# Second graph layer: one-hot matrix on ScalarE, feature halves paired on VectorE, one head-sum matmul per block, and programs written out

## The reference

```python
enh = node_features + 0.1 * query_emb[None, :]
Q = (enh @ Wq + bq).reshape(N, H, D)
K = (enh @ Wk + bk).reshape(N, H, D)
V = (enh @ Wv + bv).reshape(N, H, D)
rel = rel_w[edge_relations]
mod_k = K[src] + 0.2 * rel[:, None, :]
scores = jnp.einsum('ehd,ehd->eh', Q[dst], mod_k) / D ** 0.5
seg_max = jax.ops.segment_max(scores, dst, num_segments=N)
ex = jnp.exp(scores - seg_max[dst])
denom = jax.ops.segment_sum(ex, dst, num_segments=N)
w = ex / denom[dst]
agg = jax.ops.segment_sum(w[:, :, None] * V[src], dst, num_segments=N)
```

## Time and profile before

| | |
|---|---|
| median of 3 runs | 1894.05 us (1893.74 to 1898.3) |
| the profiled execution | 1896.89 us, span 1895.1 us |
| busy in the span | PE 88%, DVE 85%, ACT 55%, POOL 55% |
| TensorE's granted clock, mean | 0.943 of full speed |
| DMA | 333.74 MB, mean 176 GB/s |

### The profile page before, as it was taken

How to read it: one execution, slowest core, us unless ns; L and a number is a source line. 1 busy time by engine, 2 the same in 40 slices (tenths; PEclk the granted TensorE clock), 3 DMA queues, 4 the chain that set the end, 5 groups by cost and what they waited for, 6 DMA issues and landing times. The chain is left out here.

```text
span 1895.1 us, 46044 instructions
## 1 busy us (share of the span) xinstructions
PE 1660.5 (88%) x11647; PEld 1543.2 (81%) x11647; DVE 1617.6 (85%) x3652; ACT 1047.8 (55%) x2325; POOL 1040.0 (55%) x1079
## 2 busy tenths in 40 slices
PE   6979999999999999996096999889899899899844
PEld 3779999999999999996085888788788788788633
DVE  5569999999999999999874799888888788888887
ACT  1468888888888888885453444343343343343114
POOL 0056666666566666665714766565565565565164
PEclk6989999999999999998598999999999999999978
DMA  4466666666666666662227877576576576676513
GB/s 130 153 188 186 185 188 185 185 186 184 188 185 185 186 183 188 184 186 85 98 97 248 251 205 213 169 208 185 170 208 179 170 207 181 178 200 190 195 51 102
DMA packets 165698, 333.74 MB, mean 176 GB/s; under 512 B 31015, under 2 KB 101384, under 8 KB 165092
## 3 DMA queue, kind: packets, MB, share of 16 engines
q0 software_dynamic: 70400, 231.64, 42.6%
q1 hardware_dynamic: 95204, 101.16, 16.9%
HBM read 307.63 MB, written 25.06 MB: 176 GB/s over the span
## 5 line engine op out<-in xcount | busy, mean ns | idle before, releaser
L456 POOL DMA_INDIRECT gath<-edge_in_tab,idx x440 | 464.2, 1055 | 301.3 <-DVE gate_in L864 230.5
L469 POOL DMA_INDIRECT kept_more<-kv_tab,idx x176 | 173.4, 985 | 145.4 <-DVE weighted L1029 87.1
L1128 PE MATMUL bank<-w_lo,relu_hi 128*128 128x256 f32 x880 | 249.4, 283 | 0.0
L1128 PE MATMUL bank<-w_hi,relu_lo 128*128 128x256 f32 x880 | 249.3, 283 | 0.0
L1128 PE MATMUL bank<-w_hi,relu_hi 128*128 128x256 f32 x880 | 249.3, 283 | 0.0
L1128 PE MATMUL bank<-weighted,hot 128*128 128x260 f32 x880 | 238.7, 396 | 4.4 <-DVE agg L1060 4.4
L606 ACT ACTIVATE relu_hi<-bank 128x512 fp32r<-128x512 f32 x220 | 131.7, 599 | 141.6 <-PE bank L1128 141.6
L1128 PEld LDWEIGHTS bank<-weighted,hot 128*128 128x128 f32 x880 | 172.4, 197 | 34.5 <-DVE hot L1038 6.3
L1131 PE MATMUL bank<-ident,gath 128*128 128x128 f32 x880 | 168.8, 274 | 23.9 <-DVE ea_parts L851 13.3
L469 POOL DMA_INDIRECT hs<-kv_tab,idx x132 | 141.9, 1075 | 80.5 <-DVE weighted L1029 47.9
L873 DVE TENSOR_TENSOR msg<-bank,gate 128x512 f32<-128x512 f32 x220 | 152.1, 692 | 33.3 <-PE bank L1128 17.2
(11 more groups left out here) (266 smaller groups left out, 5018.9 us busy)
## 6 DMA issues: line engine op xcount, KB each, us to landing
ea_in<-in_ea SPq DMA_DIRECT2D x440, 64.0 KB
block_row<-row_tab SPq DMA_DIRECT2D x440, 64.0 KB
gath<-edge_in_tab,idx POOLq DMA_INDIRECT x440
kv_tab<-qkv_row SPq DMA_DIRECT2D x26, 258.0 KB, 2.5
edge_in_tab<-node_row SPq DMA_DIRECT2D x26, 256.0 KB, 2.0
xs<-in_x SPq DMA_DIRECT2D x1, 3328.0 KB, 15.5
rows_tab<-xs SPq DMA_DIRECT2D x1, 3328.0 KB, 9.3
rows_tab<-hs SPq DMA_DIRECT2D x1, 3328.0 KB, 10.9
```

What stands on the lines that cost most here:

```text
L456: g.indirect_dma_start(gath[:, q, i, :], None, edge_in_tab, bass.IndirectOffsetOnAxis(ap=idx[:, half, q, i:i + 1], axis=0)).then_inc(gath_ ...
L469: g.indirect_dma_start(kept(u, 0, KVW)[:, i, :], None, kv_tab, bass.IndirectOffsetOnAxis(ap=idx1[:, half, u % BATCH, i:i + 1], axis=0)).th ...
L1128: return nc.tensor.matmul(out_, lhsT=lhs, rhs=rhs, start=start, stop=stop)
```

## The change

Four things in the second layer:

- The features of each head are split in two parts of 32. The columns of Wk, bk, Wq, bq and of the relations are laid out so that half 0 of the keys holds the first parts of all four heads and half 1 the second parts. VectorE then adds half 1 to half 0 (`pair_parts`, 128x256), and `add_heads` is one matmul of 256 columns where it was two. `rel_parts` is filled by 8 instructions of 32 columns on ScalarE and on VectorE each, where it was 4 of 64.
- `hot1` is made by ScalarE in two stages, `node_distances` (Square of the difference, two instructions of 128x128, lag 16) and `one_hot1` (Relu of 1 minus it, 128x256, lag 17), as the first layer does.
- The order within a step is new: on VectorE `rescale` and `add_agg` stand directly behind `products`, then `pair_parts`, then `weight_values`. On TensorE `aggregate` stands ahead of `add_heads`. On ScalarE the copy of the scores is last, and `one_hot1` stands behind the exponents.
- The three pipelines are written out (`straight=True`); those of GpSimd and SyncE stay loops.

```diff
-FIRST_COL = HEADS * BATCH - 2
+FIRST_COL = HEADS * (BATCH - 1)
+PART = HEAD // 2
...
-            for h in range(HEADS):
-                last = s.mul(rel_parts[:, h * HEAD:(h + 1) * HEAD], rel_sb[:], 0.2)
+            for part in range(2):
+                for h in range(HEADS):
+                    last = s.mul(rel_parts[:, part * P + h * PART:part * P + (h + 1) * PART], rel_sb[:, part * PART:(part + 1) * PART], 0.2)
...
+            def node_distances(k, q):
+                b = KEEP * k + q
+                after(act, hot1_done, b - 1)
+                for i in range(2):
+                    last = s.activation(dist1[:, q % 2, i, :], iota_node[:], ACT.Square, bias=rel_col[:, ds(b, 1), i], scale=-1.0)
+                last.then_inc(dist1_done, 1)
+
+            def one_hot1(k, q):
+                b = KEEP * k + q
+                act.wait_ge(dist1_done, b + 1)
+                after(act, agg_ready, b - 1)
+                s.activation(hot1[:, q % 2, :, :], dist1[:, q % 2, :, :], ACT.Relu, bias=one_col[:], scale=-1.0).then_inc(hot1_done, 1)
...
-            pipeline(act, [(fetch_query, 0), (copy_keys, 1), (copy_scores, 2), (copy_weights, 6), (exponents, 5)], BLOCKS, KEEP)
+            pipeline(act, [(fetch_query, 0), (copy_keys, 1), (copy_weights, 6), (exponents, 5), (one_hot1, 17), (node_distances, 16), (copy_scores, 2)],
+                     BLOCKS, KEEP, straight=True)
...
+            def pair_parts(k, q):
+                b = KEEP * k + q
+                dve.wait_ge(prod_done, b + 1)
+                parts = kept(q, 0, CHUNK)
+                v.tensor_tensor(parts[:, 0, :], parts[:, 0, :], parts[:, 1, :], ALU.add).then_inc(paired, 1)
...
-            def one_hot1(k, q):
-                b = KEEP * k + q
-                after(dve, agg_ready, b - 1)
-                for i in range(2):
-                    last = v.tensor_scalar(hot1[:, q % 2, i, :], iota_node[:], rel_col[:, ds(b, 1), i], None, ALU.is_equal)
-                last.then_inc(hot1_done, 1)
...
-            pipeline(dve, [(one_hot_t, 0), (products, 2), (weight_values, 17), (one_hot1, 17), (rescale, 19), (add_agg, 19), (local_maxima, 3),
-                           (running_maxima, 4), (segment_maxima, 5)], BLOCKS, KEEP)
+            pipeline(dve, [(one_hot_t, 0), (products, 2), (rescale, 19), (add_agg, 19), (pair_parts, 2), (weight_values, 17), (local_maxima, 3),
+                           (running_maxima, 4), (segment_maxima, 5)], BLOCKS, KEEP, straight=True)
...
-                pe.wait_ge(prod_done, b + 1)
+                pe.wait_ge(paired, b + 1)
                 if turn == 0:
                     after(pe, scores_copied, g)
-                for c in range(2):
-                    at = FIRST_COL - HEADS * turn - 2 * c
-                    last = mm(bank[4][:, 0:CHUNK], adder[:, at:at + P], kept(q, 0, CHUNK)[:, c, :],
-                              turn == 0 and c == 0, turn == BATCH - 1 and c == 1)
+                at = FIRST_COL - HEADS * turn
+                last = mm(bank[4][:, 0:CHUNK], adder[:, at:at + P], kept(q, 0, CHUNK)[:, 0, :], turn == 0, turn == BATCH - 1)
...
-            pipeline(pe, [(keys_and_queries, 0), (ends_of_rows, 3), (carry_to_rows, 4), (add_heads, 1), (aggregate, 17), (weights_to_columns, 5)],
-                     BLOCKS, KEEP)
+            pipeline(pe, [(keys_and_queries, 0), (ends_of_rows, 3), (carry_to_rows, 4), (aggregate, 17), (add_heads, 1), (weights_to_columns, 5)],
+                     BLOCKS, KEEP, straight=True)
```

More of the change, by code:

```diff
@@ L181, in build @@
                     hot1 = sb(a1, "hot1", [P, 2, 2, P], f32)
+                    dist1 = sb(a1, "dist1", [P, 2, 2, P], f32)
             a3 = ExitStack()
@@ L246, in build @@
         brow_in, kept_in = sems("brow_in", BROWS), sems("kept_in", BATCH)
-        idx1_done, hot_t_done, key_ready, key_copied, query_fetched, query_ready, prod_done, scores_ready = (
+        idx1_done, hot_t_done, key_ready, key_copied, query_fetched, query_ready, prod_done, paired, scores_ready = (
             sem(n) for n in ("idx1_done", "hot_t_done", "key_ready", "key_copied", "query_fetched", "query_ready",
-                             "prod_done", "scores_ready"))
+                             "prod_done", "paired", "scores_ready"))
         far_done, steps_known, steps_out, steps_arrived = sem("far_done"), sem("steps_known"), sem("steps_out"), sems("steps_arrived", 2)
@@ L266, in build @@
         idx_seen, rel_in, rel_done, agg_zero = sem("idx_seen"), sem("rel_in"), sem("rel_done"), sem("agg_zero")
-        segments_known = sem("segments_known")
+        segments_known, dist1_done = sem("segments_known"), sem("dist1_done")
         def after(engine, signal, n):
@@ L491, in _ @@
             step(g.memset(qkv_row[:], 1.0))
-            step(g.memset(adder[0:HEAD, FIRST_COL:FIRST_COL + 1], 1.0))
-            g.memset(adder[HEAD:, FIRST_COL + 1:FIRST_COL + 2], 1.0).then_inc(consts, 1)
+            for h in range(HEADS - 1):
+                step(g.memset(adder[h * PART:(h + 1) * PART, FIRST_COL + h:FIRST_COL + h + 1], 1.0))
+            g.memset(adder[(HEADS - 1) * PART:, FIRST_COL + HEADS - 1:FIRST_COL + HEADS], 1.0).then_inc(consts, 1)
             pool.wait_ge(consts, 2)
@@ L913, in _ @@
             dve.wait_ge(rel_done, 1)
-            for h in range(HEADS):
-                last = v.scalar_tensor_tensor(rel_parts[RELS:, h * HEAD:(h + 1) * HEAD], in0=rel_sb[RELS:, :], scalar=0.2,
-                                              in1=rel_parts[RELS:, h * HEAD:(h + 1) * HEAD], op0=ALU.mult, op1=ALU.subtract)
+            for part in range(2):
+                for h in range(HEADS):
+                    cols = slice(part * P + h * PART, part * P + (h + 1) * PART)
+                    last = v.scalar_tensor_tensor(rel_parts[RELS:, cols], in0=rel_sb[RELS:, part * PART:(part + 1) * PART], scalar=0.2,
+                                                  in1=rel_parts[RELS:, cols], op0=ALU.mult, op1=ALU.subtract)
             last.then_inc(rel_done, 1)
@@ L1370, in col, with halves @@
         return np.ascontiguousarray(np.asarray(a).reshape(2, P).T)
+    def halves(a):
+        a = np.asarray(a)
+        return a.reshape(a.shape[:-1] + (HEADS, 2, PART)).swapaxes(-3, -2).reshape(a.shape)
     x = np.asarray(x)
@@ L1387 @@
         "query_col": col(L1_gnn_query_emb),
-        "wqkv": np.concatenate([np.asarray(a) for a in (L1_gnn_Wk, L1_gnn_Wv, L1_gnn_Wq)], axis=1),
-        "b_qkv": np.concatenate([np.asarray(a) for a in (L1_gnn_bk, L1_gnn_bv, L1_gnn_bq)])[None, :],
+        "wqkv": np.concatenate([halves(L1_gnn_Wk), np.asarray(L1_gnn_Wv), halves(L1_gnn_Wq)], axis=1),
+        "b_qkv": np.concatenate([halves(L1_gnn_bk), np.asarray(L1_gnn_bv), halves(L1_gnn_bq)])[None, :],
         "rel": np.asarray(L1_gnn_rel_w),
```

## The result

The changed kernel takes 1783.7 us (median of 4 runs, 1778.23 to 1786.45) against 1894.81 us (4 runs, 1893.74 to 1898.3) for the kernel before on the same chip: ratio 0.9407, 95% interval 0.9381 to 0.9433. The forecast was 1800 us, range 1776 to 1842; the gain is 111 us where 94 were expected. The profiled execution took 1783.17 us, of which the span is 1781.4.

What follows compares the result with a forecast made beforehand. TensorE led, VectorE close behind; VectorE would then set the pace. Ten rounds save 90.9 us, fill 1 and tail 3, relations cost 1.2: 1896.9 becomes 1803.2, and the median, 2.8 lower, 1800 us; range 1776 to 1842.

Steps and rivals of the forecast that it cites:

- the forecast's own case: Second layer: VectorE's chain sets the pace after the change, 1785 to 1818 us, chance 0.60.
- more gained: Rival: waits within VectorE's chain close up, a round of 20 blocks is 58.9 us, time 1781 us; chance 0.08.
- VectorE's round: VectorE's 20 blocks in the second layer: 58.9 us of work plus idle and a 0.4 us allowance, 60.8 us.
- the gathers: Rival: key gathers land too late for TensorE's key matmuls, a batch is about 32.0 us, time 1832 us; chance 0.14.
- VectorE sets the pace, TensorE second: Second-layer rounds after the change: VectorE needs 58.9 us, TensorE falls to 53.6 us.
- TensorE minus 0.43 us: TensorE's plain step: one head-sum matmul less, so it falls by 0.43 to 2.47 us.
- `pair_parts` at a pitch of 0.34: VectorE's added 128x256 addition was taken at 0.34 us a block, leaving 0.05 us saved against the removed hot1.
- ScalarE hidden: ScalarE's added hot1 work, 25.6 us a round, makes 51.6 of 60.8 us, hidden beside VectorE.
- the keys behind the exponents: ScalarE copies the next keys about 1.0 us later; 0.2 us a batch was set aside for it.
- The wait for `hot1`: Sign against the forecast: aggregate on TensorE waiting for ScalarE's hot1 over half a microsecond a batch.
- Loop closes: Writing out three second-layer pipelines removes the stalls where the loops close, 44.9 us over ten rounds.
- a stall of written-out streams: Rival: three engines stall for new instructions once a round, 6.0 us each, time about 1980 us; chance 0.05.

Runs made afterwards that it cites:

- hot_on_dve_2: Changed kernel with hot1 made on VectorE again and nothing of it on ScalarE, on an ordinary chip: 1851.5 us, ratio 0.9758 to the kernel before.
- two_matmuls_2: Changed kernel without pair_parts, two head-sum matmuls a block, on an ordinary chip: 1808.25 us, ratio 0.9532 to the kernel before.
- after_loops_2: Changed kernel with its three written-out pipelines as loops again, on an ordinary chip: 1817.01 us, ratio 0.9596 to the kernel before.
- after_dve_loop: Changed kernel with only VectorE's pipeline as a loop again, on the second slow chip: 2015.67 us, ratio 0.9891 to the kernel before.
- after_pe_act_loops: Changed kernel with the pipelines of TensorE and ScalarE as loops again, on the second slow chip: 1999.64 us, ratio 0.9818 to the kernel before.
- before_straight_2: Kernel before with only its three second-layer pipelines written out, on the second slow chip: 1996.84 us, ratio 0.9814 to the kernel before.
- before_straight: Kernel before with only its three second-layer pipelines written out, on the first slow chip: 2003.59 us, ratio 0.9788 to the kernel before.

## Why the prediction came out right, and where its sum did not

**How close it was.** 1783.7 us lies in the stated range, but 1.3 us outside the forecast's own case (1785 to 1818) and nearer to the rival "more gained" (1781). The mechanism held; one term, VectorE's round, was too large by 2.8 us, and the gathers, left out of the sum, took back 0.8. Of the signs, `pair_parts` at 0.41 us, the clock at 1.00 and VectorE above 95% (56.7 of 58.0) came true. TensorE below 90% (53.15 of 58.0, 92%), ScalarE at 80 to 85% (42.9 of 58.0, 74%) and a round of 60.8 us did not.

**The bound.** The step "VectorE sets the pace, TensorE second" holds: 56.7 busy us of 58.0 against 53.2. Without the second edit's relief, pairing is worth nothing (65.3 against 65.4), which is the prediction's first reading, "a saving on TensorE alone would end there", tested. The first slow chip agrees (2008.94 us with the pairing, 2003.59 without), for what it is worth there.

**TensorE minus 0.43 us, `pair_parts` at a pitch of 0.34, ScalarE hidden.** All as taken: 2.47 us a step, 0.34 us, and ScalarE at 42.9 us a round beside VectorE. "51.6, and less by pitch" was an upper bound; by pitch (1428.51 - 1428.10 = 0.41 for the Relu that stands at 506 ns in the earlier trace rows) it is lower by 9 us.

ScalarE's timeline there:

```profile
1427.62 0.59 ACT L691 COPY kept_more<-bank 128x512 f32<-128x512 f32 x1 [0.37 <-PE bank L1147]
1428.10 0.51 ACT L704 ACTIVATE hot<-dist,one_col 128x256 f32<-128x256 f32 x1
1428.51 0.68 ACT L697 ACTIVATE dist<-iota_node,rel_col 128x128 f32<-128x128 f32 x2
```

**The round, the step that was mis-sized.** The prediction had 58.9 us of VectorE work and 1.9 us of idle that would stay; measured are 56.7 and 1.3. The 0.05 us a block of saving was right, and yet busy time fell by 3.2 us, not by 1.0. The reason is how 59.9 was read. Busy time counts an instruction to its recorded end. Back to back, the next one starts 0.07 to 0.09 us before that end and the overlap is counted once (2.27 us, not 2.67, in the step shown above); ahead of a wait the whole end counts. Before, VectorE waited in most steps, so that 59.9 included many such ends, and they went with the waits. Counted in the two traces, VectorE has 38 gaps in the round of 65.4 us and 20 in the round of 58.0. Eighteen ends of 0.08 us are 1.4 us of the 2.2 that busy time fell too far. Of the other 0.8, some 0.6 are the same instructions recorded a little shorter, and why is not known. The distances of starts had the better number: a plain step of 2.28 us is 10 x 2.28 = 22.8 a batch, and with the prediction's own 5.4 for the scan chain 28.2. In the changed kernel the chain measures 5.14 us a batch more than plain steps (the three scan steps take 3.84, 3.79 and 4.35 us against 2.28 each), and the rescaling step and small waits take some 1.1. That is 29.0, and a round is 58.0. The same error explains both misses on the ordinary chip: `hot_on_dve_2`, 65.2 a round where 66.6 was expected, and in part `two_matmuls_2`, 61.0 against 63, where TensorE turned out to be busy 60.6 of 61.1.

The rival "more gained" (58.9 us a round, 1781) gave nearly the measured time, but its reason, that the waits within the chain close up, is only a part of it: 0.21 us is left behind a rescaling where 0.40 was the earlier trace rows, which is 0.4 us a round. The 0.4 us a round that the forecast set aside for the keys behind the exponents does not show: VectorE waits for copied keys only three times from 1130 to 1650.

**Gathers.** This rival was present in small. Its price was worked out from a chain of 7.9 us with a gather landing 4.4 us after its start. The chain of what ended last passes through a gather at least nine times from 1130 to 1650. Here are the first three (start us, duration, what), and TensorE and VectorE behind the middle one:

```profile
1160.05 5.52 DMA xs<-kv_tab,idx
...
1216.01 5.41 DMA xs<-kv_tab,idx
...
1280.18 5.70 DMA xs<-kv_tab,idx
```

```profile
1221.46 0.44 PE L1150 MATMUL bank<-ident,xs 128*128 128x128 f32 x2 [1.48 <-DMA xs<-kv_tab,idx]
...
1223.02 0.69 DVE L984 TENSOR_TENSOR xs<-bank,xs 128x512 f32<-128x512 f32 x1 [0.70 <-ACT xs L691]
```

TensorE waits 1.48 us, VectorE for what follows from it 0.70. Not each of them costs: the batches with these three took 29.1, 30.0 and 29.5 us, an undisturbed one 29.0. The ten rounds took 59.2, 58.2, 59.4, 58.5, 58.1, 59.8, 58.0, 59.5, 58.3 and 59.4 us. Against ten of 58.0 that is 8 us in all, an upper bound for the gathers, not the 32 of the rival. (The rival's own price is loose: its chain of 11.0 us over four steps is 2.75 us a step, not 2.65 to 2.7.)

**The wait for `hot1`.** The prediction called more than half a microsecond a batch a sign against it. It is 1.4 us a batch, the longest 1.7, and as far as the waits show it costs nothing: VectorE's additions, which need those sums, wait 0.2 us for TensorE in nine rounds. ScalarE and TensorE at the exponents:

```profile
1440.42 0.42 ACT L718 ACTIVATE e_row<-ln_sb 40x256 f32<-40x256 f32 x1 [4.22 <-DVE ln_sb L1048]
1440.80 0.50 ACT L704 ACTIVATE hot<-dist,one_col 128x256 f32<-128x256 f32 x1
...
1441.35 1.14 PE L1147 MATMUL bank<-weighted,hot 128*128 128x260 f32 x4 [1.74 <-ACT hot L704]
```

ScalarE stands in its own queue for 4.2 us until VectorE's scan chain is done, with `one_hot1` behind that wait. TensorE waits with it, but VectorE, which both wait for in the end, doesn't. The sign was badly chosen: it names a wait on an engine that no longer bounds.

**Loop closes.** 44.9 us predicted; 44.4 and 39.6 us measured on the two slow chips, none on the ordinary one, where the changed kernel shows 33. That their stalls end with the loops is shown; that on an ordinary chip they are worth 44.9 to the kernel before rests on the earlier trace rows and its ten rounds. In the trace of `after` GpSimd and SyncE, whose loops stayed, have no more than 0.3 us between a branch that leads back and what follows. The written-out streams show no stall in the changed kernel from 1130 to 1650: no "issue" wait over 0.5 us stands on VectorE, none on TensorE's matmuls, and the only long one on ScalarE (2.1 us) stands behind the late gather shown above.

One reading of the prediction was wrong. The stretch from 1137.6 to 1203.0 of the earlier trace rows is not written out. VectorE enters its loop at 1137.7, and the branch that closes it stands there nine times, first at 1203.1, and leads back eight times:

```profile
L296 DVEq COMPARE_BRANCH  x9: 55/63/63, 1203.1 to 1772.8; - x9
L296 DVEq FUSED_REGOPS  x8: 74/74/80, 1207.0 to 1706.2; - x8
```

So 65.4 us is the loop's first pass, before any close; the second stretch, 6.0 us longer, holds the close at 1203.1. The written-out round is the one ahead of it, 63.8 us between two additions to `agg`. As evidence against a stall of written-out streams the prediction had that round, not this one; the argument for the 44.9 us stands, since the first pass has no close in it either.

**Relations, fill and tail.** The relations' eight shorter instructions on VectorE take 1.9 us where four took 1.1: +0.8, forecast +1.2. The fill gave 4.6 us in all where 1 - 1.2 was forecast; 1.8 us of it fall before the first product, and why was not tried. Of the 1.8 us, 1.3 had gone before the second layer's first gather. The tail gave 0 of 3 us. From the first to the last of its last ten additions it is 10.5 us instead of 11.6, the last still with a wait of 0.52 us for TensorE; the ten steps ahead of them take 24.2 us instead of 23.0, with waits for TensorE of 1.77 and 2.22 us. No experiment looked into it. Together these terms gave 4.6 + 0 - 1.3 = 3.3 us where 2.8 was forecast.

So 110.5 us in ten rounds against 90.9: 2.8 us a round too little gain forecast in VectorE's time, less 0.8 us a round, at most, for gathers that were left out.

## What to carry to other kernels

To find the floor of an engine that waits now and won't later, add up the start-to-start distances of a step that has no gap in it; busy time of a stretch with waits is too high (here by 2.2 us of 58.9). Where two engines are within a few per cent of each other, price an edit for the one only together with what relieves the other: apart, one of the edits here was worth 0.1 us a round, together it was worth 2.2. A wait counts only on the engine that sets the pace (TensorE's 1.4 us a batch for `hot1` left VectorE waiting 0.2 us in nine rounds): look there first, and then ask who behind the waiting engine has a lead.

## What the runs showed of the hardware

**In these traces only VectorE's loop over the blocks stalls at its close.** In the trace of `before`, its eight closes (L296) have a gap between the branch and the next instruction of 3.3 to 4.25 us, in `after_loops_2` of 3.2 to 4.1 and in `after_dve_loop` of 3.4 to 4.3. The trace of `before` has 436 instructions of VectorE's stream in one pass: 278 of its sequencer (registers, semaphores, branches), which don't count as busy, and the 158 of the earlier trace rows. ScalarE's stream, with 160, has a gap of 0.2 us there, TensorE's, with 490 in its sequencer and weight loads, 0.06 to 0.10, and VectorE's own shorter loops of the same kernel, with 11 to 64, 0.14 to 0.24. In `after_pe_act_loops` ScalarE's body has 298 and its gap is still 0.20 to 0.23. So the length alone doesn't separate them, even if TensorE's f32 work, which is recorded twice (x4 for two matmuls in the earlier trace rows), is counted once (some 490 again, its matmuls included). What decides, no run tells.

**On two of three chips TensorE's signals seem to have arrived late.** VectorE (with releaser "remote") and ScalarE at one moment of `before_straight_2`, on the second slow chip:

```profile
1454.36 1.04 PE L1128 MATMUL bank<-weighted,hot 128*128 128x260 f32 x4
1455.71 0.36 PE L1128 MATMUL bank<-hot_more,rel_parts 128*128 128x256 f32 x1
1457.54 0.70 DVE L1029 TENSOR_TENSOR weighted<-xs,weight_col 128x520 f32<-128x520 f32 x1 [2.24 <-remote]
1457.55 0.58 ACT L687 COPY kept_more<-bank 128x512 f32<-128x512 f32 x1 [2.30 <-PE bank L1128]
```

Both engines are released at 1457.5, by two different semaphores, though TensorE's work for them had ended 1.5 us and more before. Waits of L1029 with the releaser "remote" take 55.7 us of 600 there (53.0 us in `before_straight`, on the first slow chip); the kernel before on the ordinary chip has none. If signals are late there, a kernel whose engines depend on each other in every step would pay for it whatever its busy times are, and that would explain why everything but the writing out gained nothing there. It is an explanation from one view, not tested; the cause is open. It isn't the whole either: the same kernel's first addition to `agg` came at 1132.6 us instead of 1073.9, 59 us late, although from 100 to 800 us only 13 us of waits have that releaser.

**Behind a gap of 2.2 us the clock was 1.00, behind gaps of 2.4 us both 1.00 and 0.67.** The stretch of `after_loops_2` right behind the close shown above, where TensorE had been idle for 2.24 us (columns as in the earlier trace rows):

```profile
1259.40:1264.60 5.20, 5.18 (x32) 4.48 (x33) 5.20 (x12) 2.93 (x7) 3.02 (x4) 1.00 0.78 224
```

The granted clock is 1.00 in 5.2 us that begin with the matmul behind the gap; in the kernel before, TensorE was idle for 3.81 us at a close, and in the 5.2 us behind it the clock was 0.50. Over all eight closes the length of the gap doesn't separate the two. In `after_loops_2` the clock of such 5.2 us is 1.00 behind gaps of 2.24, 3.11, 2.37 and 2.42 us, and 0.67 behind 2.42, 2.39, 2.38 and 2.58 us. In `before` it is 0.50 behind six gaps of 3.46 to 4.24 us, 0.71 behind 3.32 and 0.67 behind 3.80.
